# Down biases of a mixture-of-experts layer added as the products leave PSUM, with a new written-out order

## The chip, the cores and the metric

The kernel runs on one core of one Trainium2 chip. A time is the device time of one execution in microseconds (us). The kernel before has three timed executions, with a median of 795.2 us. The engines are TensorE (PE, with its weight loads as PEld), VectorE (DVE), ScalarE (ACT), GpSimd (POOL) and SyncE (SP), which here issues most of the transfers.

## The reference, cut to what matters

A two-layer block on x of 16 sequences, 256 rows each, 128 channels. Layer 0 is attention and a mixture of experts, layer 1 a gated recurrence, a gated feed-forward network and a channel mixer. The change lies in the experts (`I` is 512, `E` is 8, two experts a row):

```python
scores = sigmoid(xf @ gate_w + bias)
top_scores, top_idx = top_k(scores, K)
top_scores = top_scores / (sum(top_scores) + 1e-06)
w = zeros((T, E)).at[arange(T)[:, None], top_idx].add(top_scores)
hact = gelu(einsum('th,ehi->tei', xf, up_w) + up_b)
eo = einsum('tei,eih->teh', hact, down_w) + down_b
combined = einsum('teh,te->th', eo * 0.1, w)
shared = (gelu(xf @ sw_up + sb_up) @ sw_down + sb_down) * 0.1
out = shared + combined
out = out / (max(abs(out)) + 1e-06)
```

## The kernel before, in words

The 4096 rows are 8 chunks of 512. The program has four stages.

1. Attention, chunk by chunk, with the second layer norm, the routing and the scatter of rows to the experts of the chunks that are done. It ends where DVE writes the last residual (`woh`, L1333); SP waits for it before it loads anything late.
2. Expert tiles 0 to 16. A tile is 256 rows of one expert. SP fetches its up and down weights and its rows (`fetch`, L2037 to L2049: buffers WU, WD and XT, six of each); PE transposes the rows (`xt`, L1065) and DVE copies them; four `up` products (L1079), four GELUs (ACT L1784), four `down` steps of two products (L1098); DVE copies the result out of PSUM (`ev`, L1539), and POOL stores it. The shared expert of chunk 0 runs at the start of this stage.
3. Expert tiles 17 to 38. The up weights and rows are split in two (`wsh` and `xs` on DVE, `wsl` on POOL, L1941), and an `up` step is three products (L1085 to L1087).
4. Rest: POOL gathers the expert rows of a chunk back (`gather`, L1963, four steps one after the other), DVE sums and normalizes them (`cmb`, `fin1`), PE transposes (`fin2`, L1113), and layer 1 of that chunk follows. The shared expert of chunks 1 to 7 (`up` L1075, `down` L1098) lies between, as work that waits for no gather.

The shared expert's PSUM bank of a chunk also collects all down biases. `rows` transposes the chunk's routing weights, with a column of ones, to nine rows (L1057: four transposes, copied by ACT at L1772), and after the last `down` step four products over these nine rows (L1105) add the eight expert biases, weighted, and the shared bias. DVE then copies the bank (L1535).

The order is written out. Each program step is a stage of a job; `arrange` reads the strings ORDER1 (stages 1 and 2) and ORDER2 (stage 4), two characters a step, and puts the steps down in that order; each engine runs its own in that order. Stage 3 is written by a loop. While it reads, `arrange` replays the steps with the durations in HELD, the delays in HOPS and BEHIND, and lets `fill` put idle products (L855, no one reads them) where it sees PE too little busy.

Of the kernel before, what the change touches and what calls it, by code (L numbers as in the profile page):

```python
# [7 lines left out]
F = mybir.dt.float32  # L8
R = mybir.dt.float32r
B16 = mybir.dt.bfloat16  # L10
ALU = mybir.AluOpType
# [5 lines left out]
CH = 512  # L17
# [21 lines left out]
def constants():  # L39
# [48 lines left out]
    "up": ("PE", 0.858, None), "rows": ("PE", 0.436, None), "down": ("PE", 0.888, None), "ev": ("DVE", 0.6, None),  # L88
# [18 lines left out]
BEHIND = {"PE": 0.165, "ACT": 0.115, "DVE": 0.08, "POOL": 0.045, "SP": 0.0}  # L107
# [7 lines left out]
def cost(name, key):  # L115
    engine, held, table = HELD["t_" + name if key[:1] == ("t",) else name]
    if name == "mxr" and key[2] == 0:
        held = 0.845
    if name == "causal" and key[1] > 3:
        held = 1.19  # L120
    if name == "pv" and key[2]:
        held = 0.44
    if name == "down" and key[0] == "s" and key[2] == 3:
        held = 1.776
    return engine, held, table
# [29 lines left out]
    "GpG4F2GwGpF3GvGwGpG1GpGvG5GwG5GpGpG6GvG2F3G6GxGqGpG6G7GqG7G9G7G9G6GpGuG3G8G7G+G8G-G+G8G-F3G+G8G-HBG+GzHAG-G8HBHAG8GuGvHC"
    "HAHDHCHAHDF3HCG0HEHDHFHCHEHDHAHEHAHFGuHGHEHHHGG1HIHHGrHGHIHHHJHGHIHHHIHJGvHEG2HKHIHEGvHLHKHIHMHLGrHKHMHLHNHKHNHMHLHOHMHP"
# [153 lines left out]
def schedule():  # L310
# [126 lines left out]
    def plan(n):  # L437
# [3 lines left out]
        if n:  # L441
            yield stage("plan_rows", after=[("woh", NB - 1)])
# [1656 lines left out]
```

## Time and profile before

| what | value |
|---|---|
| three timed executions | 793.75, 795.2, 796.96 us |
| the profiled execution | 796.7 us |
| its span, first to last instruction | 795.0 us |
| mean granted clock of PE | 0.971 |
| busy: PE, DVE, ACT, POOL | 730.2, 502.4, 498.3, 387.8 us |

### The profile page before, as it was taken

The numbers are of one execution on the slowest core, as the hardware profiler recorded it, in microseconds if no ns is written. First come the engines' busy times: TensorE is split into PE (matmuls) and PEld (weight loads), VectorE is DVE, ScalarE is ACT, GpSimd is POOL, SyncE is SP. The second block draws the span as 40 slices with busy tenths as digits, with TensorE's granted clock in tenths as the row PEclk, the third lists the DMA queues.
The fourth block names the chain that finished last, engine by engine and source line by source line (L and its number), as shares of the span: only waits on it lengthen the run. The fifth ranks groups of instructions, "written<-read, shape, count | busy, mean of one in ns | idle before, by whom it ended". The sixth has DMA issues, their size and how long they took to land.

```text
span 795.0 us, 12566 instructions
## 1 busy us (share of the span) xinstructions
PE 730.2 (92%) x3768; PEld 442.7 (56%) x3768; DVE 502.4 (63%) x1906; ACT 498.3 (63%) x749; POOL 387.8 (49%) x563
## 2 busy tenths in 40 slices
PE   4889899899889998988999899998999999999994
PEld 3444445444544544446789899986545644434442
DVE  3387888879984889784912345513346495795652
ACT  1749675775838556655455455552688886688563
POOL 7327444664856277653451355534445465522243
PEclk9999998999999989899999999998999999999998
DMA  9990000000000000005767667711000101000012
GB/s 280 380 369 29 1 1 0 18 12 14 14 24 4 2 28 24 3 15 168 231 214 214 179 204 233 208 40 31 26 25 23 31 22 32 20 1 0 1 40 66
DMA packets 59855, 64.18 MB, mean 81 GB/s; under 512 B 6474, under 2 KB 42668, under 8 KB 59788
## 3 DMA queue, kind: packets, MB, share of 16 engines
q1 hardware_dynamic: 53410, 49.84, 20.3%
q0 software_dynamic: 6320, 13.53, 5.4%
q8 instruction: 30, 0.49, 0.3%
q14 instruction: 37, 0.30, 0.1%
q10 hardware_dynamic: 58, 0.02, 0.0%
HBM read 35.18 MB, written 28.18 MB: 80 GB/s over the span
## 4 chain that ended last, share of the span: by engine, by line
PE 61%; DVE 15%; issue 8%; POOL 6%; ACT 6%; DMA 3%; SPq 0%; DVEq 0%; POOLq 0%; ACTq 0%
PE PS L1098 11%; DVE JK L1290 6%; PE PS L1079 4%; PE PS L952 3%; PE PS L990 3%; PE PS L1161 3%; PE PS L895 3%; PE PS L1154 3%; PE PS L1168 2%; PE PS L901 2%; POOL got L1963 2%; PE PS L907 2%; DMA got<-expert_out,IG 2%; PE PS L975 2%; PE PS L961 2%
## 5 line engine op out<-in xcount | busy, mean ns | idle before, releaser
L1290 DVE CUSTOM_DVE_ANT_0 JK<-PS,CM 128x256 bf16<-128x256 f32 (+1 forms) x512 | 148.9, 352 | 23.3 <-PE PS L952 21.9
L1784 ACT ACTIVATE GF<-PS,XN 128x256 f32<-128x256 f32 x156 | 73.7, 475 | 67.1 <-PE PS L1087 37.4
L1098 PE MATMUL PS<-WD,GF 128*128 128x128 f32 x624 | 94.9, 276 | 0.9 <-ACT GF L1784 0.6
L952 PE MATMUL PS<-KZ,QS 128*128 128x512 f32 x192 | 87.2, 506 | 5.5 <-DVE MX L1290 3.0
L1963 POOL DMA_INDIRECT got<-expert_out,IG x64 | 63.6, 993 | 54.4 <-DMA got<-expert_out,IG 38.2
L1098 PEld LDWEIGHTS PS<-WD,GF 128*128 128x128 f32 x624 | 85.9, 192 | 6.4 <-ACT GF L1784 1.9
L1935 POOL DMA_INDIRECT expert_rows<-five,IU x64 | 63.1, 986 | 50.2 <-DMA expert_rows<-five,IU 20.4
L1738 ACT ACTIVATE PA<-PS 128x1024 f32<-128x1024 f32 x64 | 64.1, 1029 | 21.7 <-PE PS L975 21.4
L1922 POOL TENSOR_SCALAR_AFFINE_SELECT PA<-PA 128x256 f32<-128x256 f32 x128 | 50.0, 420 | 52.1 <-ACT PA L1738 50.7
L1885 POOL TENSOR_SCALAR H<-xc,MOD 128x256 f32<-128x256 f32 x56 | 32.9, 598 | 79.4 <-DVE xc L1259 79.3
L952 PEld LDWEIGHTS PS<-KZ,QS 128*128 128x128 f32 x192 | 35.6, 197 | 43.9 <-DVE MX L1290 20.7
L1946 POOL DMA_DIRECT2D expert_out<-YT x39 | 21.7, 557 | 68.8 <-DVE YT L1539 68.1
L1922 POOL TENSOR_SCALAR_AFFINE_SELECT PB<-PB 128x512 f32<-128x512 f32 x64 | 39.5, 645 | 18.9 <-ACT PB L1740 18.7
L1290 DVE DVE_READ_ACCUMULATOR2_ANT MX<- 128x1 f32 x512 | 42.3, 83 | 0.0
L1079 PE MATMUL PS<-XS,WU 128*128 128x256 f32 x136 | 41.2, 385 | 1.0 <-DVE XN L1535 0.5
L1606 DVE SCALAR_TENSOR_TENSOR hf<-PS,V,GF 128x512 f32<-128x512 f32 x32 | 23.7, 745 | 28.1 <-PE PS L1161 25.4
L1098 PEld LDWEIGHTS PS<-five,GF 128*128 128x128 f32 x256 | 33.8, 196 | 11.8 <-issue 10.8
L1740 ACT ACTIVATE PB<-PS 128x1024 f32<-128x1024 f32 x32 | 32.5, 1027 | 7.2 <-PE PS L977 5.8
L895 PE MATMUL PS<-X,CT 128*128 128x512 f32 x64 | 35.4, 636 | 1.5 <-DVE X L1333 1.4
L901 PE MATMUL PS<-sq,CT 128*128 128x512 f32 x58 | 32.4, 644 | 4.4 <-DVE MX L1290 1.8
L990 PE MATMUL PS<-PA,VA 128*32 128x512 f32 x256 | 34.3, 629 | 2.2 <-DVE MX L1290 0.5
L1539 DVE COPY YT<-PS 128x256 f32<-128x256 f32 x39 | 16.5, 424 | 31.1 <-PE PS L1098 31.1
(295 smaller groups left out, 1741.6 us busy)
## 6 DMA issues: line engine op xcount, KB each, us to landing
expert_rows<-five SPq DMA_DIRECT2D x16, 1024.0 KB, 12.8
WU<-in_L_ffn_up_w SPq DMA_DIRECT2D x39, 256.0 KB, 2.9
WD<-in_L_ffn_down_w SPq DMA_DIRECT2D x39, 256.0 KB, 3.1
XT<-expert_rows SPq DMA_DIRECT2D x39, 128.0 KB, 3.2
expert_out<-YT POOLq DMA_DIRECT2D x39, 128.0 KB
PA<-in_L_attn_x SPq DMA_DIRECT2D x8, 256.0 KB, 5.5
out<-yo SPq DMA_DIRECT2D x8, 256.0 KB, 2.3
expert_rows<-five,IU POOLq DMA_INDIRECT x64
```

What stands on the lines that cost most here:

```text
L895: pe.matmul(bank("lc", c, s), centre, chunk(X, c), start=True, stop=True).then_inc(sems["cen"], 1)
L901: pe.matmul(bank("ln_var", c, s), mean, sq_of("sq", c, s), start=True, stop=True).then_inc(sems["var"], 1)
L952: pe.matmul(bk.rearrange("p (j n) -> p j n", n=wd), q, ks, start=True, stop=True).then_inc(sems["mx_mm"], 1)
L990: m = pe.matmul(o, VA[:, 2 * b % 8, j, :], p0[:, j, 2 * h:2 * h + 2, :], start=True, stop=False)
L1079: pe.matmul(bk[:, 0:TR], WU[u % NF][:, f], XS[slot["xs", u]][:, :], start=True, stop=True).then_inc(sems["up"], 1)
L1098: m = pe.matmul(bk[:, b], g[:, b], wd[:, k, :], start=(k == 0 and t == 0), stop=(k == 3 and t == TB - 1 and kind == "t"))
L1290: m = dve.tensor_tensor_reduce(JK[n % 2][:, s], bk[:, s], CM[:, 256 - wd:256] if wd == 128 else CM[:, 0:256], -1.0, 3.0e38, ALU.add, ALU.m ...
L1738: m = act.activation(PT0[b % 2][:, j:j + 2, g:g + 2, :].rearrange("p j g n -> p j (g n)"), two(both), ACT.Exp, scale=SCALE)
L1784: act.activation(GF[slot["gf", kind, u, k]][:, 0:n], bank("up", kind, u, k)[:, 0:n], ACT.Gelu, bias=bias).then_inc(sems["gelu"], 1)
L1922: m = pool.affine_select(out=a, in_=a, pattern=[[0, 2 if u < 4 else 4], [1, 128]], compare_op=ALU.is_ge, fill=zero, base=0, channel_multip ...
L1935: pool.indirect_dma_start(out=XD[:, :], out_offset=bass.IndirectOffsetOnAxis(ap=IU[:, c, n, k:k + 1], axis=0), in_=HT[c % 2][:, k, :], in_ ...
L1963: pool.indirect_dma_start(out=got[b][n][:, k, :], out_offset=None, in_=YD[:, :], in_offset=bass.IndirectOffsetOnAxis(ap=IG[:, n, 4 * c + k ...
```

## The change

The nine rows go: `rows`, its ACT copy, the four products over them, their buffers WT and DB. Each expert tile gets a buffer BD, six in all: `fetch` loads the expert's down bias, the same 512 bytes to each of 128 partitions, between WD and XT, and the tile's semaphore counts to 64 in place of 48. `ev` adds BD as it leaves PSUM. The shared bias is loaded once in the same way (SD), ahead of the late weights, and the shared `ev` adds it. A fetch waits for the `ev` of the tile six before, which was a wait for its last `down`. Both order strings are new, and BEHIND holds 0.25 for PE, which was 0.165, and 0.12 for ACT, which was 0.115.

```diff
-BEHIND = {"PE": 0.165, "ACT": 0.115, "DVE": 0.08, "POOL": 0.045, "SP": 0.0}
+BEHIND = {"PE": 0.25, "ACT": 0.12, "DVE": 0.08, "POOL": 0.045, "SP": 0.0}
...
-    "H3H5H2H5H4H3H6H4H7H6H4G2H8H7H4H6H8H7H6H8H7H8H8G3H8"
+    "H6H4H6H4H4H4H6H6H7H7H7H7G4H8H8H8H8G2GzG0G1H8H8G3"
...
-            yield stage("plan_rows", after=[("woh", NB - 1)])
+            yield stage("plan_rows", after=[("woh", NB - 1), ("rt_out", NCH - 1)])
...
-                        + ([("down", "t", t - NF, 3)] if t >= NF else []))
+                        + ([("ev", "t", t - NF)] if t >= NF else []))
...
-                if k == 1:
-                    yield stage("rows", c, takes=[(ring, "rows", (c,), ("rw", c)), (WTS, "wts", (c,), ("down", "s", c, 3))])
...
-                            after=[("gelu", "s", c, k)] + [("load_late",)] * (k == 3))
+                            after=[("gelu", "s", c, k)])
...
-        yield stage("ev", "s", c, after=[("down", "s", c, 3)])
+        yield stage("ev", "s", c, after=[("down", "s", c, 3), ("load_late",)])
...
-    WT = [sb(f"WT{k}", [9, CH]) for k in range(2)]
-    DB = sb("DB", [9, 128])
+    SD = sb("SD", [128, 128])
+    BD = [sb(f"BD{k}", [128, 128], where=moe) for k in range(NF)]
...
-            if kind == "s" and k == 3:
-                w.wait_ge(*at("rw", u))
-                w.wait_ge(ld_db, 32)
-                for t in range(4):
-                    b = slice(128 * t, 128 * t + 128)
-                    m = pe.matmul(bk[:, b], WT[slot["wts", u]][:, b], DB[:, :], start=False, stop=(t == 3))
+                              stop=(k == 3 and t == blocks - 1))
...
-                dve.tensor_copy(chunk(XN, u), bank("down", kind, u)).then_inc(sems["ev"], 1)
+                w.wait_ge(ld_sd, 16)
+                dve.tensor_tensor(shared(u), bank("down", kind, u).rearrange("p (k d) -> p k d", d=128),
+                                  SD[:, :].unsqueeze(1).to_broadcast([128, 4, 128]), ALU.add).then_inc(sems["ev"], 1)
...
-            dve.tensor_copy(YT[u % 3][:, :], bank("down", kind, u)[:, 0:TR]).then_inc(sems["ev"], 1)
+            dve.tensor_tensor(YT[u % 3][:, :].rearrange("p (k d) -> p k d", d=128),
+                              bank("down", kind, u)[:, 0:TR].rearrange("p (k d) -> p k d", d=128),
+                              BD[u % NF][:, :].unsqueeze(1).to_broadcast([128, TB, 128]), ALU.add).then_inc(sems["ev"], 1)
...
-            sp.dma_start(DB[0:8, :], i["L0_ffn_down_b"]).then_inc(ld_db, 16)
-            sp.dma_start(DB[8:9, :], i["L0_ffn_sb_down"].rearrange("(a p) -> a p", p=128)).then_inc(ld_db, 16)
+            sp.dma_start(SD[:, :], i["L0_ffn_sb_down"].partition_broadcast(128)).then_inc(ld_sd, 16)
...
-                w.wait_ge(*at("down", "t", t - NF, 3))
+                w.wait_ge(*at("ev", "t", t - NF))
...
+            sp.dma_start(BD[k][:, :], i["L0_ffn_down_b"][bass.ds(ex, 1)].rearrange("o h -> (o h)").partition_broadcast(128)
                         ).then_inc(ld_t[k], 16)
```

The order moves on every engine. Three places follow. A row is a line of the program, the operation, what it writes and reads, and its shape; "x4" stands for four in a row. Line numbers are lower by 4 to 23 in the kernel after.

First, PE from the shared `up` and `down` steps of chunk 3 to the first `fin2` (the one that reads `on`), while the first gather is under way. Before:

```order
L1098 MATMUL PS<-five,GF 128x128 x4
L1075 MATMUL PS<-H,five 128x512
L1057 MATMUL PS<-CT,WS 9x128 x4
L1098 MATMUL PS<-five,GF 128x128 x4
L1075 MATMUL PS<-H,five 128x512
L1098 MATMUL PS<-five,GF 128x128 x4
L1105 MATMUL PS<-DB,WT 128x128 x4
L1075 MATMUL PS<-H,five 128x512
L1113 MATMUL PS<-CT,on 128x128 x4
```

After:

```order
L1085 MATMUL PS<-five,GF 128x128 x4
L1062 MATMUL PS<-H,five 128x512
L1085 MATMUL PS<-five,GF 128x128 x4
L1062 MATMUL PS<-H,five 128x512
L1085 MATMUL PS<-five,GF 128x128 x4
L1062 MATMUL PS<-H,five 128x512
L1094 MATMUL PS<-CT,on 128x128 x4
```

Between the last tile and the first `fin2` PE had 12 `up` and 8 `down` steps, three times the nine-row transposes and two times the nine-row products; it now has 13 `up` and 9 `down` steps.

Second, SP at the change from the second to the third stage, from the fetch of tile 17 (buffer 5) to the next one. Before:

```order
L2044 DMA WU5<-in_L0_ffn_up_w 128x512
L2045 DMA WD5<-in_L0_ffn_down_w 128x4x128
L2049 ISA
L2049 DMA XT5<-expert_rows 128x256
L2042 TENSOR_LOAD XN
L2042 ISA x2
L2043 TENSOR_LOAD XN
L2043 ISA x2
L2044 ISA
L2044 DMA WU0<-in_L0_ffn_up_w 128x512
```

After:

```order
L2021 DMA WU5<-in_L0_ffn_up_w 128x512
L2022 DMA WD5<-in_L0_ffn_down_w 128x4x128
L2024 ISA
L2024 DMA BD5<-in_L0_ffn_down_b 128x128
L2028 ISA
L2028 DMA XT5<-expert_rows 128x256
L2019 TENSOR_LOAD XN
L2019 ISA x2
L2020 TENSOR_LOAD XN
L2020 ISA x2
L2021 ISA
L2021 DMA WU3<-in_L0_ffn_up_w 128x512
```

The fetch that follows that of tile 17 was that of tile 18 (buffer 0); it is now that of tile 21 (buffer 3), and those of tiles 18, 19, 20 and 22 come behind it. The fetch of tile 21 waits for tile 15.

Third, PE where the tiles begin, from the weight transposes (`gates`) to the first expert `up` (the one that reads `WU`). Before:

```order
L1122 MATMUL PS<-CT,gates 128x128 x2
L1098 MATMUL PS<-five,GF 128x128 x4
L1122 MATMUL PS<-CT,gates 128x128 x4
L1065 MATMUL PS<-CT,XT 128x128 x2
L1098 MATMUL PS<-five,GF 128x128 x4
L1105 MATMUL PS<-DB,WT 128x128 x4
L1079 MATMUL PS<-XS,WU 128x256
```

After:

```order
L1103 MATMUL PS<-CT,gates 128x128 x2
L1052 MATMUL PS<-CT,XT 128x128 x2
L1021 MATMUL PS<-gate,H 128x8 x4
L1030 MATMUL PS<-CT,H 128x128 x4
L1103 MATMUL PS<-CT,gates 128x128 x4
L1066 MATMUL PS<-XS,WU 128x256
L1085 MATMUL PS<-five,GF 128x128 x4
L1066 MATMUL PS<-XS,WU 128x256
```

Three of the four shared `down` steps of chunk 0 now lie between the `up` steps of tile 0, and the routing of chunk 7 lies ahead of them. Over the whole program `fill` puts 18 idle products in the place of 50.

## Rows read from the trace of the kernel before

**Rows 1.** Windows: span, busy time (instructions) per engine, PE clock, DMA share, GB/s

```profile
0.00:361.50 361.50, 320.81 (x1728) 167.46 (x1728) 279.73 (x1422) 229.14 (x331) 203.47 (x355) 0.96 0.20 67
480.00:500.00 20.00, 20.00 (x178) 20.00 (x177) 10.20 (x24) 10.92 (x23) 10.58 (x12) 1.00 0.79 235
528.00:552.00 24.00, 21.50 (x118) 14.44 (x116) 5.02 (x15) 9.30 (x15) 10.24 (x11) 0.97 0.13 37
552.00:586.00 34.00, 31.53 (x135) 19.63 (x135) 12.63 (x28) 22.30 (x27) 12.96 (x15) 0.87 0.09 24
586.00:795.00 209.00, 196.93 (x586) 94.12 (x584) 131.92 (x239) 150.11 (x200) 93.19 (x104) 0.99 0.08 24
```

**Rows 2.** The page: the chain that ended last, by engine

```profile
PE 61%; DVE 15%; issue 8%; POOL 6%; ACT 6%; DMA 3%; SPq 0%; DVEq 0%; POOLq 0%; ACTq 0%
```

**Rows 3.** Timeline of PE in stage 4: start, duration, line, tiles, records

```profile
605.98 1.05 PE L1098 MATMUL PS<-five,GF 128*128 128x128 f32 x8
606.97 1.15 PE L1105 MATMUL PS<-DB,WT 9*128 9x128 f32 x8
...
609.01 1.02 PE L1075 MATMUL PS<-H,five 128*128 128x512 f32 x2
609.87 1.02 PE L1147 MATMUL PS<-bz,WL 128*128 128x512 f32 x2
610.73 1.05 PE L1098 MATMUL PS<-five,GF 128*128 128x128 f32 x8
611.62 1.02 PE L1168 MATMUL PS<-hf,WL 128*128 128x512 f32 x2
...
618.10 0.60 PE L1057 MATMUL PS<-CT,WS 128*9 128x128 f32 x4
618.54 1.02 PE L1154 MATMUL PS<-XN,WL 128*128 128x512 f32 x2
```

**Rows 4.** Timeline of PE as the first gather ends

```profile
548.37 1.13 PE L1075 MATMUL PS<-H,five 128*128 128x512 f32 x2
552.34 1.12 PE L1113 MATMUL PS<-CT,on 128*128 128x128 f32 x4 [2.84 <-DVE on L1570]
```

**Rows 5.** Timeline of SP: fetch issues in stage 2, and of tile 21

```profile
371.93 0.34 SPq L2044 DMA_DIRECT2D WU<-in_L_ffn_up_w  x1
372.39 0.38 SPq L2045 DMA_DIRECT2D WD<-in_L_ffn_down_w  x1
...
374.65 0.33 SPq L2044 DMA_DIRECT2D WU<-in_L_ffn_up_w  x1
...
447.33 0.36 SPq L2049 DMA_DIRECT2D XT<-expert_rows  x1
```

**Rows 6.** Issue to landing of the row fetches XT

```profile
DMA to landing us min/median/max: 2.9/3.2/4.1
```

**Rows 7.** Timeline of PE: the rows of tile 18

```profile
452.23 0.63 PE L1065 MATMUL PS<-CT,XT 128*128 128x128 f32 x2
```

**Rows 8.** Groups of instructions: the idle products

```profile
L855 PE MATMUL PS<-CT 128*128 128x128 f32 x100 | 18.9, 299 | 0.0
```

**Rows 9.** Windows: a stretch of attention at the lower clock

```profile
130.00:135.00 5.00, 3.94 (x8) 2.23 (x9) 4.03 (x20) 2.62 (x5) 2.76 (x7) 0.58 0.00 0
```

**Rows 10.** Groups of instructions on DVE by form

```profile
L1539 DVE COPY YT<-PS 128x256 f32<-128x256 f32 x39 | 16.5, 424 | 31.1 <-PE PS L1098 31.1
L1521 DVE TENSOR_TENSOR XL<-PS,XH 128x256 fp32r<-128x256 f32 x22 | 9.3, 424 | 0.8
L1276 DVE TENSOR_TENSOR qt<-PS,CT 128x512 f32<-128x512 f32 x8 | 5.5, 686 | 5.7 <-PE PS L915 5.7
L1535 DVE COPY XN<-PS 128x512 f32<-128x512 f32 x8 | 5.5, 684 | 17.4 <-PE PS L1105 17.4
```

**Rows 11.** SP's waits for PE: total, times, longest

```profile
SPq L2042 <- PE PS L1098: 30.1, 27, 6.3
```

**Rows 12.** The page: the software queue's packets, MB, share of 16 engines

```profile
q0 software_dynamic: 6320, 13.53, 5.4%
```

More of the change, by code:

```diff
@@ L87 @@
     "plan_rows": ("DVE", 4.9, None), "fetch": ("SP", 2.9, None), "load_late": ("SP", 3.0, None), "tw": ("PE", 0.4, None),
-    "up": ("PE", 0.858, None), "rows": ("PE", 0.436, None), "down": ("PE", 0.888, None), "ev": ("DVE", 0.6, None),
+    "up": ("PE", 0.858, None), "down": ("PE", 0.888, None), "ev": ("DVE", 0.6, None),
     "gelu": ("ACT", 0.57, "gelu"), "t_up": ("PE", 0.434, None), "t_gelu": ("ACT", 0.36, "gelu"), "t_down": ("PE", 0.444, None),
@@ L298 @@
     "pl_ei": "plan_tiles", "pl_ub": "plan_bias", "pl_ix": "plan_rows", "pl_w": "plan_rows",
-    "rw_tp": "rows", "rw": "rows", "xt_tp": "xt", "xs": "xs", "w_hi": "wsh", "w_lo": "wsl", "up": "up", "gelu": "gelu", "down": "down", "ev": "ev",
+    "xt_tp": "xt", "xs": "xs", "w_hi": "wsh", "w_lo": "wsl", "up": "up", "gelu": "gelu", "down": "down", "ev": "ev",
     "cmb": "cmb", "fin": "fin1", "fin_bk": "fin2", "moe_x": "fin3", "cen": "lc",
@@ L316, in schedule @@
     LT, LH, LL, LN = (Ring(range(2)) for _ in range(4))
-    GF, WTS, XS, WS2 = Ring(range(6)), Ring(range(2)), Ring(range(2)), Ring(range(2))
+    GF, XS, WS2 = Ring(range(6)), Ring(range(2)), Ring(range(2))
     def stage(name, *key, takes=(), after=()):
@@ L1049, in dpm @@
             m.then_inc(sems["dp_mm"], 1)
-        def rows(c):
-            w.wait_ge(*at("wst", c))
-            w.wait_ge(zeroed, 4)
-            for e in prior["rows", c]:
-                w.wait_ge(*at(*e))
-            for k in range(4):
-                m = pe.transpose(bank("rows", c)[0:9, 128 * k:128 * k + 128], WS[:, c, k, :], ident)
-            m.then_inc(sems["rw_tp"], 1)
         def xt(t):
-            w.wait_ge(ld_t[t % NF], 48 * (t // NF + 1))
+            w.wait_ge(ld_t[t % NF], 64 * (t // NF + 1))
             for e in prior["xt", t]:
@@ L1765, in hta @@
             act.activation(HT[c % 2].rearrange("p k d -> p (k d)"), bank("ht", c), ACT.Copy).then_inc(sems["ht"], 1)
-        def rows(c):
-            w.wait_ge(*at("rw_tp", c))
-            w.wait_ge(*at(*att_done))
-            for e in prior["wts", c]:
-                w.wait_ge(*at(*e))
-            act.activation(WT[slot["wts", c]][:, :], bank("rows", c)[0:9, :], ACT.Copy).then_inc(sems["rw"], 1)
         def gelu(kind, u, k):
```

106 lines of the change are left out of this document (52 added, 54 removed).

## The prediction

> **What bounds the kernel now.** I read the windows by stage first. In stage 4, from 586 us, PE is busy for 196.93 of 209 us, DVE for 131.92 and ACT for 150.11 [rows 1]; stage 3 is full too, 20.00 of 20. The reader is to see that these stretches are paid for in PE time: what PE has less to do there comes off the end, unless something else comes late. Attention is looser: PE 320.81 of 361.5 us, and DVE 279.73 [rows 1]. The chain that ended last says the same, 61% over PE [rows 2]. Between 528 and 552 us PE has shared work only while the first gather runs, and then stands 2.84 us for the normalized rows of chunk 0 [rows 4]. The clock goes with such stands: 0.58 of full speed in 130 to 135 us [rows 9], a mean of 0.87 over the 34 us behind the first gather [rows 1].
>
> **What a chunk's nine rows cost PE.** A shared `down` step followed by another kind of product takes 0.89 us from start to start (610.73 to 611.62), a 512-column product 0.86 (609.87 to 610.73) [rows 3]. With the nine-row products between, `down`, nine rows and the next product take 609.01 - 605.98 = 3.03 us; without them it would be 0.89 + 0.86 = 1.75. So the four products cost 1.28 us, not just their own 1.15, since the neighbours on both sides are drawn out. The four transposes cost 618.54 - 618.10 = 0.44 [rows 3]. One chunk is 1.72 us, eight are 13.8.
>
> **Stage 4.** Seven chunks lie here, 12.0 us. Two products and three sets of transposes stood ahead of the first `fin2`, 3.9 us of cover for the gather. The new order puts one more `up` (0.86) and one more `down` (0.89) in, so cover falls by 2.1 us and the stand grows from 2.84 [rows 4] to about 5: no gain and no loss, the gather sets that time. Behind it five products and four sets of transposes go, 5 x 1.28 + 4 x 0.44 = 8.2, and the two steps moved ahead, 1.75. That is -9.9 us. What hid nothing there hides nothing now: after the work of PE the next in line is ACT, at 150.11 of 209 [rows 1]. The ends: -12.0 if every part counts; -4 if PE starves behind the first gather, where it already had 2.5 us idle of 34 [rows 1] and now has some 6 us less shared work to fill in.
>
> **Start of stage 2.** One set of nine rows, 1.72 us, goes from between the end of attention and the tiles. Tile 0's fetch is now the first of its kind rather than the second, but the new transfer stands ahead of its rows, and the second layer norm and routing of chunk 7 stand ahead of its first `up` on PE. I take -1.7, between -4 (a whole fetch of 2.72 us, 371.93 to 374.65 [rows 5], gained as well) and +2 (that much lost to chunk 7, less the nine rows).
>
> **Change to stage 3: a wait is added.** SP now fetches tile 21 ahead of tile 18. In the trace the rows of tile 21 are issued at 447.33, behind tile 15 [rows 5]. The new fetch starts some 0.5 later (it waits for `ev`, a copy of 0.42 [rows 10] with its signal, and not for the last `down`), has one more issue of 0.46 (371.93 to 372.39), and only then comes tile 18's, 2.72 + 0.46 = 3.18 [rows 5]: rows issued at 451.5, landed 3.2 later [rows 6], 454.7. PE transposed them at 452.23 [rows 7]. Behind that transpose stand the last two `up` steps and all `down` steps of tile 17, and `wsh` on DVE and `wsl` on POOL wait for the same load. So PE stands 2.5 us: +2.5. It is 0 if the gap that is already there before tile 17 reaches over it, 3.5 if the split of the weights comes late too. The fetches of tiles 19 and 20 follow at 3.2 us, and PE takes a tile per 3.4 us (12 `up`, 16 `down` and 2 transpose records make 30; 178 records in 20 us [rows 1]), so they only just arrive.
>
> **The two additions that I cost at nothing.** DVE: the copy out of PSUM takes 424 ns for 256 columns and 684 for 512; an addition of a PSUM and an SBUF operand 424, and with a broadcast middle dimension 686 [rows 10]. SP and the transfers: SP waited 27 times for PE ahead of a fetch, 30.1 us, 1.1 a time [rows 11]; the new issue and the later signal take about 1.0 of it, and a fetch is six tiles ahead. The DMA engines are busy 0.79 of 3.37 us a tile [rows 1], 2.66 us. A tile moves 768 KB in 896 pieces (WU 128, WD 512, XT 128, YT 128); 64 KB in 128 pieces more is 0.22 by bytes, 0.38 by pieces, so at most 3.04 of 3.37. What hides it is gone if a piece costs as one of the software queue, 5.4% of 16 x 795 us over 6320 [rows 12], 109 ns: 0.87 a tile, 3.53 in all, 0.16 over, times 22 tiles +3.5 us. I take 0.
> The Trainium skill ("DMA: Bandwidth & Descriptors", section "Bandwidth") speaks against the transfer: in its words, "Transfers under 64 KB are descriptor-dominated", and this one is just at that size, in rows of 512 bytes. Its rule would put the sum nearer the end of +3.5 us, the row of bytes nearer 0; it is the third rival.
>
> **Attention.** No part of the nine rows is here; only the order and the idle products change. In the trace the 50 idle products make 100 records [rows 8]; two records are a quarter of the 0.89 us of a `down` step, 0.22 us. 32 fewer are 7.0 us of PE if none stood in a gap, and 0 if all did. PE has 40.7 us without work in attention [rows 1], so a better order has room, and the order says nothing of what it does on the chip. I take -3, with -12 (a third of that gap) and +12 (below) as ends.
>
> **The sum.** -9.9 - 1.7 + 2.5 - 3 + 0 = -12.1. Against the profiled execution, 796.7 us: 784.6. That execution is 1.5 above the median of 795.2, so for the median 783.1; I say 783.5. The likeliest case alone runs from 776 to 789.
>
> **Rivals.**
> First, the one on the other side: the clock. The idle products go from 50 to 18, and each longer stand in attention is followed by a stretch at 1.2 GHz. 130 to 135 us lost 0.42 x 5 = 2.1 us [rows 9], and such a stretch has its ends in the neighbouring windows, so up to 3.4. If six more such stretches come, that is up to +20: 803.5. It decides from about four more (13.6 us eat up the -12.1). For it: the mean clock is already 0.96 there with the idle products. Against: most of them stand in small gaps, and they go where the planner sees none.
> The Trainium skill ("TensorE: Matmul & The Clock Gate", section "HAM oscillation — how this bites in real kernels") has it that an array which idles between bursts of work is throttled anew and pays at the half clock; by that this rival has the mechanism, and the stretch at 0.58 agrees.
> Second, stage 4 is bound by the gathers and by the chain of a chunk for longer, so that the shared work is missed: the -9.9 shrinks to -4 and the sum to -6, 789. For: PE waits for the first gather now. Against: from 586 us on it waits for nothing.
> Third, the biases' transfers fill the DMA engines, or the new fetch order costs again at each tile 18 to 20: +3.5, 787. For: 0.79 busy. Against: six buffers.
> Fourth, the new order is worth in attention and behind the first gather what its room allows: -12 there, and 2 more: 772.
>
> **Chances.** Forecast 0.57, clock 0.13, gathers 0.13, transfers 0.04, better order 0.13. A measurement of this kernel tells 0.5%, 4 us, from no change. Faster than 791.2: nearly all of the forecast, three in four of the second and third rival, all of the fourth, 0.78; I lower it to 0.75, as an order is hard to judge from its rows. Within 0.5%: 0.12. Slower than 799.2: 0.13. The range runs from 773 to 798: it leaves out half of the fourth rival and most of the first.
>
> **What would show it.** Right: no records of nine-row products or transposes; stage 4 from the last tile to the end shorter by about 10 us, with PE still full behind some 590 us; the stand before the first `fin2` near 5 us; DVE additions at 424 and 686 ns; a stand of 2 to 3 us at the transpose of tile 18; tiles of stage 3 still at 3.4 us. Wrong: attention longer by more than 4 us with more windows below a clock of 1; idle PE between 560 and 620 us; SP without waits and the DMA share near 1 in stage 3; or the stages each as said but attention by 10 us shorter.

## The result, and the profile after

The changed kernel takes 772.1 us (median; single executions 762.7 to 774.0) against 796.0 us (the profiled execution of 796.7 us counted in), a ratio of 0.968 (95% interval 0.961 to 0.975). Executions over 1.5% above the shortest of their kernel are left out of every ratio below, among them one of the changed kernel in r4 that took 1139.3 us at a mean granted clock of 0.557, for which nothing here gives a cause. The forecast was 783.5 with a range of 773 to 798: the direction was right, the gain of 24 us is twice the 12.1 forecast, and the median lies just below the range. The profiled execution is the shortest one, 762.7 us with a span of 760.9, so its stages are set below beside those of other executions.

The windows of the changed kernel: attention; tiles 17 to 38; shared work until the first `fin2`; the 34 us behind it; the rest; and 20 us of stage 3. Columns as in [rows 1].

```profile
0.00:334.20 334.20, 302.43 (x1671) 155.98 (x1671) 284.38 (x1424) 226.84 (x331) 204.27 (x355) 0.99 0.22 73
426.30:506.90 80.60, 77.37 (x659) 77.17 (x660) 35.67 (x84) 41.69 (x88) 38.87 (x42) 0.96 0.73 216
506.90:532.40 25.50, 19.21 (x99) 12.62 (x98) 4.70 (x15) 8.24 (x12) 10.24 (x11) 0.95 0.12 32
532.40:566.00 33.60, 31.55 (x131) 19.63 (x132) 13.17 (x28) 24.17 (x31) 16.65 (x19) 0.94 0.10 28
566.00:760.90 194.90, 183.70 (x522) 86.94 (x520) 131.65 (x238) 135.25 (x186) 91.00 (x99) 0.99 0.09 25
480.00:500.00 20.00, 20.00 (x177) 20.00 (x176) 9.95 (x24) 10.94 (x24) 10.54 (x13) 1.00 0.67 199
```

Attention ends at 334.2 instead of 361.5 us [rows 1], with VectorE busy for 284 us (280 before). PE is busy there for 18.4 us less and idle for 31.8 us instead of 40.7. The chain of the page (before: [rows 2]) has moved towards VectorE, which answers for 22% in place of 15%:

```profile
PE 56%; DVE 22%; issue 7%; ACT 5%; DMA 4%; SPq 2%; POOL 2%; DVEq 0%; ACTq 0%; POOLq 0%
```

The stages of both profiled executions, in us. Attention ends with VectorE's last residual; stage 3 runs from the second product of tile 17 (0.2 us behind the first, where the window above begins) to the last `down` of tile 38.

| | attention | stage 2 | stage 3 | shared work to first `fin2` | rest | span |
|---|---|---|---|---|---|---|
| before | 361.5 | 89.9 | 76.8 | 24.2 | 242.6 | 795.0 |
| after | 334.2 | 92.3 | 80.4 | 25.5 | 228.5 | 760.9 |
| forecast of the difference | -3 | -1.7 | +2.5 | -9.9 for the last two together | | -12.1 |
| measured | -27.3 | +2.4 | +3.6 | +1.3 | -14.1 | -34.1 |

Three single rows of the forecast can be read directly. The first two are on PE (timeline, columns as in [rows 4, 7]): the rows of tile 18, then the first `fin2`.

```profile
430.48 0.69 PE L1052 MATMUL PS<-CT,XT 128*128 128x128 f32 x2 [3.23 <-DMA XT<-expert_rows]
...
532.37 1.11 PE L1094 MATMUL PS<-CT,on 128*128 128x128 f32 x4 [6.29 <-DVE on L1556]
```

PE stands 3.23 us for tile 18 (2.5 forecast) and 6.29 us ahead of the first `fin2` (5 forecast). The SP timeline gives the reason for the first as it was forecast: the fetch of tile 21 is issued first, that of tile 18 behind it, and its rows land after 430 us.

```profile
423.87 0.33 SPq L2028 DMA_DIRECT2D XT<-expert_rows  x1
...
427.06 0.33 SPq L2028 DMA_DIRECT2D XT<-expert_rows  x1
```

The groups of instructions answer to [rows 8] and [rows 10]: the idle products have 36 records, not 100; the two additions take 424 and 683 ns, as the copies did.

```profile
L851 PE MATMUL PS<-CT 128*128 128x128 f32 x36 | 6.9, 338 | 0.0
...
L1523 DVE TENSOR_TENSOR YT<-PS,BD 128x256 f32<-128x256 f32 x39 | 16.5, 424 | 46.5 <-PE PS L1085 46.5
...
L1518 DVE TENSOR_TENSOR XN<-PS,SD 128x512 f32<-128x512 f32 x8 | 5.5, 683 | 3.9 <-PE PS L1085 3.8
```

The hardware queue of the page carries 59152 packets, where it had 53410; 39 x 128 = 4992 of the 5742 more are the tiles' biases:

```profile
q1 hardware_dynamic: 59152, 52.46, 22.8%
```

### The profile page after: what moved, and what is told of

It reads as the page before. It is cut to its first block, busy times and chain, and to the rows that moved or that the text cites. A ratio compares the mean times of both kernels' runs of the same rounds, so it can differ in the third digit from the quotient of the medians.

```text
span 760.9 us, 12350 instructions
## 1 busy us (share of the span) xinstructions
PE 696.3 (92%) x3608; PEld 424.0 (56%) x3608; DVE 505.9 (66%) x1906; ACT 481.8 (63%) x734; POOL 388.6 (51%) x562
## 3 DMA queue, kind: packets, MB, share of 16 engines
q1 hardware_dynamic: 59152, 52.46, 22.8%
## 4 chain that ended last, share of the span: by engine, by line
PE 56%; DVE 22%; issue 7%; ACT 5%; DMA 4%; SPq 2%; POOL 2%; DVEq 0%; ACTq 0%; POOLq 0%
PE PS L1085 9%; DVE JK L1271 8%; PE PS L948 4%; PE PS L1135 3%; PE PS L891 3%; PE PS L986 3%; PE PS L1066 3%; PE PS L1149 3%; PE PS L1142 3%; PE PS L897 2%; PE PS L903 2%; PE PS L988 2%; PE PS L911 1%; DMA got<-expert_out,IG 1%; PE PS L1072 1%
## 5 line engine op out<-in xcount | busy, mean ns | idle before, releaser
L1724 ACT ACTIVATE PA<-PS 128x1024 f32<-128x1024 f32 x64 | 64.7, 1026 | 15.2 <-PE PS L971 14.1
L1900 POOL TENSOR_SCALAR_AFFINE_SELECT PA<-PA 128x256 f32<-128x256 f32 x128 | 49.8, 419 | 27.9 <-ACT PA L1724 27.3
L1924 POOL DMA_DIRECT2D expert_out<-YT x39 | 21.7, 558 | 80.3 <-DVE YT L1523 80.3
L1523 DVE TENSOR_TENSOR YT<-PS,BD 128x256 f32<-128x256 f32 x39 | 16.5, 424 | 46.5 <-PE PS L1085 46.5
L1900 POOL TENSOR_SCALAR_AFFINE_SELECT PB<-PB 128x512 f32<-128x512 f32 x64 | 38.9, 635 | 16.4 <-ACT PB L1726 16.2
L1085 PEld LDWEIGHTS PS<-five,GF 128*128 128x128 f32 x256 | 34.7, 198 | 14.1 <-issue 12.7
L1653 ACT ACTIVATE sq<-PS 128x512 f32<-128x512 f32 x28 | 16.7, 599 | 31.4 <-PE PS L891 31.2
L1534 DVE SCALAR_TENSOR_TENSOR XN<-got,W,XN 128x128 f32<-128x128 f32 x64 | 20.8, 386 | 21.8 <-DMA got<-expert_out,IG 21.5
L1085 PE MATMUL PS<-five,GF 128*128 128x128 f32 x256 | 35.0, 281 | 0.0
```

What stands on the lines that cost most here:

```text
L1085: m = pe.matmul(bk[:, b], g[:, b], wd[:, k, :], start=(k == 0 and t == 0), stop=(k == 3 and t == blocks - 1))
L1724: m = act.activation(PT0[b % 2][:, j:j + 2, g:g + 2, :].rearrange("p j g n -> p j (g n)"), two(both), ACT.Exp, scale=SCALE)
L1900: m = pool.affine_select(out=a, in_=a, pattern=[[0, 2 if u < 4 else 4], [1, 128]], compare_op=ALU.is_ge, fill=zero, base=0, channel_multip ...
```

## The experiments

Theory A: most of the gain is the new order of attention; the biases and the other orders nearly cancel. Theory B: the nine rows are what was gained. Each table of orders is changed as a whole; of such a diff the first line pair stands here, and the words say what it does. The kernel before was timed with each group of runs (797.0, 797.3, 799.9, 798.9 and 797.3 us), and ratios are to it.

**r1, the changed biases with the old order.**

```diff
-BEHIND = {"PE": 0.25, "ACT": 0.12, "DVE": 0.08, "POOL": 0.045, "SP": 0.0}
+BEHIND = {"PE": 0.165, "ACT": 0.115, "DVE": 0.08, "POOL": 0.045, "SP": 0.0}
...
-    "AFAAAAAAAAABAGAGABACAAAAAAABADABAEABABABAAAAAGAGAHAHAAAAAAAKAKAGAGAGABABALALANANAGANANAMAMAMAMAJABABAJABAHAHAPAPAQAQAOAO"
+    "AAAAACABAFAAABADAAAAABAEABAGAGABAAAAAKABALABAAAKAGALABAIAAAJAGAAAIAJAGAAABAHAAAIAGAHAGANAIAGAMANANABAMANAMAHABATAHAMABAP"
```

> The changed biases, with the order of the kernel before (its steps of the nine rows taken out, its planner numbers kept, so 36 fill steps with 60 idle products where the kernel before has 50 with 100). Theory A (most of the gain is the new order in attention, some 27 us of the two profiled executions): attention ends within 5 us of the 361.5 us of before, stage 4 is shorter by about 10 us, and the time is about 785 us. Theory B (the removal of the nine rows is worth most, the order little): about 775 us. If idle products cost PE time (rival C), attention is shorter by up to 9 us too (40 fewer products of 0.22 us).

(The counts of idle products there are wrong: the kernel before has 35 steps with 50 products, recorded as 100, and this one 36 steps with 60.) Measured: 787.8 us, ratio 0.990 (0.982 to 0.998), some 8 us. The profiled execution took 800.9 us, 13 more than the median, and attention ends at 372.9 us in it, not within 5 us of 361.5 as expected; most of that is a slow start and the clock (below). Stage 3 takes 76.8 us as before, though every tile fetches its bias, so the transfer costs nothing. Behind the first `fin2` it takes 236.0 us instead of 242.6: the five chunks of nine rows there are worth 6.6 us, not the 8.2 forecast, and 1.7 of the 6.6 are the clock (a stretch of 3.4 us at 1.2 GHz that the kernel before has at 581 us does not come).

**r2, the old attention in the changed kernel; r3, the new attention in the kernel before.** r2 exchanges the table up to the residual of block 15 and the planner numbers, r3 the same the other way round (the diff of r1 in reverse, on the kernel before).

> The changed kernel with the old order up to the end of attention, the new order behind it. Theory A: attention ends near 361 us again, the time is 772 + 20 to 27 = 792 to 799 us. Theory B: within 5 us of the changed kernel, 767 to 777 us. The stage behind the last tile keeps the 254 us of the changed kernel by both.

> The kernel before (biases as products over nine rows) with the new order up to the end of attention, the old order behind it; 9 fill steps in place of 50. Theory A: attention ends at 334 to 340 us, the time is 796 - 20 to 27 = 769 to 776 us. Theory B: 790 us or more. What lies behind attention keeps its 433.5 us (361.5 to 795.0) by both.

Measured: r2 792.1 us, ratio 0.989 (0.978 to 1.000), attention 367.6 us in the profiled execution; r3 773.5 us, ratio 0.969 (0.960 to 0.978), attention 334.9. Both times lie where theory A puts them. (The 50 steps in r3's expectation are 35.) r3 has none of the change of the biases and has its whole gain. Its windows, attention and all from the last tile's last `down` on:

```profile
0.00:334.90 334.90, 301.60 (x1671) 155.58 (x1671) 283.30 (x1423) 226.77 (x331) 204.44 (x356) 0.99 0.22 73
...
505.30:771.90 266.60, 249.70 (x835) 128.00 (x833) 149.63 (x280) 181.69 (x242) 116.19 (x129) 0.97 0.09 25
```

The last part is the 266.8 us of before. (Of the expectation's 433.5 us behind attention it takes 437.0; the 3.5 more lie in stage 2.) Theory A holds, B falls.

**r4, the changed kernel again.** No edit.

> The changed kernel once more, word for word, since its executions lie up to 11 us apart (762.7 to 774.0). If one stage is what varies, the profile shows it: a time near 772 us with attention ending some 9 us later than 334 us means that it is attention and its clock; a later stage longer by 9 us means that it is that one.

Measured: 768.9 us. The profiled execution is 8.0 us longer than the first one, and attention is 7.4 us longer (341.6), with stretches at the lower clock of 27.3 us in all where the first had 6.8. What differs between these two executions lies in attention.

**r11, all new orders, with the nine rows.**

```diff
-BEHIND = {"PE": 0.165, "ACT": 0.115, "DVE": 0.08, "POOL": 0.045, "SP": 0.0}
+BEHIND = {"PE": 0.25, "ACT": 0.12, "DVE": 0.08, "POOL": 0.045, "SP": 0.0}
...
-    "AAAAACABAFAAABADAAAAABAEABAGAGABAAAAAKABALABAAAKAGALABAIAAAJAGAAAIAJAGAAABAHAAAIAGAHAGANAIAGAMANANABAMANAMAHABATAHAMABAP"
+    "AFAAAAAAAAABAGAGABACAAAAAAABADABAEABABABAAAAAGAGAHAHAAAAAAAKAKAGAGAGABABALALANANAGANANAMAMAMAMAJABABAJABAHAHAPAPAQAQAOAO"
```

> All new orders (attention, tiles, fetches, the second layer), with the biases of the shared expert as products over nine rows as before. If the parts add up (measured so far, in profiled executions: attention -17 to -27, stage 2 +2.4, stage 3 +4, the last part -8 of its -14), the time is 770 + 6 to 9 = 776 to 779 us, and the bias change by itself is worth 6 to 9 us. Rival: the nine rows fill gaps before the first gather and chunk 0 and are worth 3 us at most, 770 to 773.

Measured: 770.0 us, ratio 0.961 (0.954 to 0.969), against 0.968 and 0.961 of the changed kernel. In the new order the change of the biases can't be told from nothing: the rival is right. Its windows from the last tile on, until the first `fin2` and behind it:

```profile
512.80:536.80 24.00, 23.11 (x127) 15.57 (x125) 4.63 (x15) 8.37 (x14) 10.24 (x11) 1.00 0.12 35
536.80:768.70 231.90, 220.72 (x708) 111.41 (x708) 144.20 (x266) 161.85 (x221) 107.21 (x118) 0.99 0.09 25
```

Ahead of the first `fin2` PE is idle for 0.9 us of 24.0, at the full clock, where the changed kernel is idle for 6.3 of 25.5. No stretch at the lower clock follows, where the changed kernel has one of 6.8 us (0.95 ahead of the first `fin2`, 0.94 over the 34 us behind it). In this order the nine rows filled that gap. The whole part is 255.8 us with them and 254.0 without: without them PE is busy for 9.3 us less there, but idle for 7.5 us more (19.5 against 12.0).

**Where attention gains: r9, the new order up to block 4; r10, the new order from there on.** Both are the kernel before with the old order behind attention. r9 has the first lines of r11's diff, the new planner numbers with them; r10 keeps the old numbers:

```diff
-    "CMCzCyCcCzCNCbCNCaCZCyCODFDEC1COCyCZCyCPCcC0C1CPA-CPC0CgCPAIC0C1AIDJCgCZC1CgCaC0DdC2CfDJA-DdC4C3C4DdDGC3CfC+DdDGCfC6DIDH"
+    "CMCzCyCcCzCNCbCNCaCZCyCODFDEC1COCyCZCyCPCcC0C1CPA-CPC0CgCPAIAIDcDcDdDdDdDcDcBxBxC1C1C0C0CZC2BxBxDdCaCvCvC3C3DJDJDeDeC4C4"
```

> The kernel before with the new order up to the residual of attention block 4 (about 160 us), and the old order of all that is left behind it. By then the new order has started 646 instructions on VectorE where the old one has 582. Theory of the head start (what is brought forward on VectorE early is harvested at the end of attention): 797 - 8 to 15 = 782 to 789 us. Rival (the gain accrues where the order is denser, and the first 160 us are the part without a gain): within 4 us of the kernel before, 793 to 801 us.

> The counterpart: the kernel before with the old order up to the residual of block 4, the new order from there to the end of attention, the old one behind it. Head start: 797 - 8 to 15. Rival: nearly all of it, 797 - 18 to 23 = 774 to 779 us.

Measured: r9 789.7 us, ratio 0.987 (0.979 to 0.996); r10 792.3, ratio 0.988 (0.979 to 0.996). Each half is worth 8 to 10 us, the whole 23. r9's gain of 10 us is the size that the theory of the head start gave, and the rival (the first 160 us bring nothing, the rest nearly all) falls in both runs. In the profiled executions attention ends at 351.6 us in r9, 9.9 sooner than in the kernel before; 6.8 of these are the clock (13.7 us at 1.2 GHz instead of 27.3) and 3.6 idle time of PE. In r10 it ends at 361.5, as before, but with 41.0 us at the lower clock; that execution (796.4 us) is also 4 us above r10's median.

**r14, the changed kernel with the old planner numbers**, which choose banks and idle products.

```diff
-BEHIND = {"PE": 0.25, "ACT": 0.12, "DVE": 0.08, "POOL": 0.045, "SP": 0.0}
+BEHIND = {"PE": 0.165, "ACT": 0.115, "DVE": 0.08, "POOL": 0.045, "SP": 0.0}
```

> The changed kernel with its orders and the old planner numbers (0.165/0.115), which give 426 of its 1685 buffers another place and 8 idle-product steps instead of 7. If the order is the cause: 768 to 774 us, attention within 5 us of 334 to 341. If the choice of banks is: towards 790.

Measured: 765.3 us, ratio 0.956 (0.949 to 0.963), attention 338.8. It is the order, not the banks: the time is not above the changed kernel's.

**The idle products: r5, none in the changed kernel; r6, 48 instead of 18; r13, none in the kernel before.** r5 and r13 share the first edit.

```diff
 def fill(P, banks, done, busy, since, until, own):
+    return until
```

```diff
-WINDOW, LEAST, WORST, MOST, ONE, SPARE = 3.4, 0.6, 0.5, 2, 0.215, 0.1
+WINDOW, LEAST, WORST, MOST, ONE, SPARE = 3.4, 0.7, 0.65, 3, 0.215, 0.1
```

> The changed kernel without any idle products (7 steps with 18 products go). If an idle product only costs its time (0.22 us each), attention ends up to 4 us sooner and the time is 766 to 770 us. If the idle products hold the clock (the rival of the prediction), attention shows two or more further stretches of 7 us at half the clock and the time is 775 us or more.

> The changed kernel with the planner's thresholds for idle products raised (0.6/0.5/2 to 0.7/0.65/3), the order of all other work kept: 36 steps with 48 products, about as many as the kernel before has (35 with 50). If part of what attention gained is that 32 idle products went, it is longer by up to 7 us (775 to 779); if they stand in gaps and hold the clock, it is 765 to 771.

> The kernel before without its 50 idle products. If they cost their time (0.22 us each, with the neighbours), it is faster by up to 11 us, 786 to 792; if they fill gaps and hold the clock, slower by 4 us or more, 801 to 810, with more than 27 us at half the clock in attention. From the changed kernel (18 products taken out moved nothing) I expect within 4 us of 797.

Measured: r5 772.9 us, ratio 0.967 (0.962 to 0.973); r6 767.1, ratio 0.961 (0.956 to 0.966); r13 807.3, ratio 1.007 (1.002 to 1.011). In the profiled executions r5 has 41.0 us at the lower clock in attention, r6 6.8. Taking all 50 out of the kernel before costs 5 us by the ratio and 8 by the medians: the second case of the expectation, and my "within 4 us" falls. Its 34.1 us at the lower clock alone would not show why, since r10 has 41.0 with 36 idle products, but the mean granted clock of all executions does: 0.948 to 0.961 without them, 0.963 to 0.980 for the kernel before timed beside it. In the changed kernel neither direction leaves the spread of its own executions, but r5 and r6, timed together, do not overlap: four executions of 770.3 to 775.1 us at clocks of 0.957 to 0.969 without idle products, four of 765.7 to 768.0 at 0.979 to 0.981 with 48. That is r6's second case, while r5 falls between its two, and it is about 6 us for 48 idle products here too. So 32 fewer idle products are not what gained 23 us, and the premise of the clock rival, that they hold the clock, is right in both kernels.

**r7 and r16, the fetch of tile 21 behind those of 18 to 20.** One table line; the letter pairs `Gz` and `G0` to `G3` are the fetch jobs.

```diff
-    "H6H4H6H4H4H4H6H6H7H7H7H7G4H8H8H8H8G2GzG0G1H8H8G3"
+    "H6H4H6H4H4H4H6H6H7H7H7H7G4H8H8H8H8GzG0G1G2H8H8G3"
```

> The changed kernel with the fetch of tile 21 behind those of tiles 18 to 20 again. By the step of the prediction the stand of 3.2 us at the transpose of tile 18 goes, and with it perhaps the low-clock stretch behind it: the stretch of tiles 17 to 38 falls from 80.4 to 81.1 us to about 77, the time by 3 to 4 us, to about 768. Rival: the stand comes back at tile 21, and nothing is gained.

> The fetch order's repair alone once more, on the chip of r15: 760 to 764 us. If r15 is within 2 us of it, the repair of the late weights is worth nothing in the whole, though its stage got 4 to 5 us shorter.

Measured: r7 761.6 us, ratio 0.953 (0.947 to 0.958); r16 764.3, ratio 0.956 (0.949 to 0.962). Stage 3 in r7 and the transpose of tile 18, which now waits for nothing:

```profile
433.60:508.90 75.30, 75.30 (x659) 75.29 (x659) 35.20 (x83) 41.61 (x88) 39.07 (x42) 1.00 0.72 209
```

```profile
434.16 0.38 PE L1052 MATMUL PS<-CT,XT 128*128 128x128 f32 x2
```

75.3 us (76.5 in r16) against 80.4 and 81.1 in the changed kernel, whose order costs 4 to 5 us here: the stand and a stretch at the lower clock behind it. Of the two, r16 (expected 760 to 764) is the second timing of the same kernel, so the repaired kernel is at 762 to 764 us, where 768 was expected.

**r8, the first fetch ahead of the late weights, and the transposes of those weights behind tile 1; r12, this and the fetch order; r15, r12 with the idle products of r6; r17, all fetches in the order of the tiles, the late weights behind the fetch of tile 1.** The jobs moved are `Gs` (late weights) and `Gv` (their transposes). r8:

```diff
-    "GSGSGRGRGtF0F0F0F0GjGkGjGjGkGkGTGTGmGmGlGlGTGTFDGnGnF1F1F1GnGnF1F1F1F1F1F3F3GoGwGwGoGoGyGyGsGzG0G3G1G2F2F2GoGoGoGwGwGwGv"
+    "GSGSGRGRGtF0F0F0F0GjGkGjGjGkGkGTGTGmGmGlGlGTGTFDGnGnF1F1F1GnGnF1F1F1F1F1F3F3GoGwGwGoGoGyGyGzGsG0G3G1G2F2F2GoGoGoGwGwGwGy"
```

> The changed kernel with the first tile's fetch ahead of the late weights on SP, and the transposes of those weights on PE behind tile 1. The fetch of tile 0 is then issued at about 334 rather than 341 us, and the stands of 2.3 and 2.6 us on PE at 344 and 347 us go: 4 to 5 us less, up to 8 if the low-clock stretch at 345 to 352 goes too; 765 to 768 us. Rival: the same products wait for chunk 7's routing instead, and under 2 us are gained.

> The changed kernel with both repairs: fetches in order for tiles 18 to 21, and the first tile's fetch ahead of the late weights. If they add (about -8 and -5), 757 to 760 us, with tiles 0 to 16 at 87 us and tiles 17 to 38 at 75 to 77. Rival: they free the same wait, 762.

> Both repairs, and 48 idle products rather than 18. If the idle products only steady the clock, 758 to 763 us and a narrower spread than the 8.7 us of r12; if they cost, 765 or more.

> The changed kernel with all fetches in the order of their tiles and the late weights behind the fetch of tile 1 (the transposes of those weights behind tile 1 on PE, as in r8). If the stand at tile 1 was what the repair still cost, tiles 0 to 16 take 84 to 85 us (87.1 in r8, 92.0 in the changed kernel), tiles 17 to 38 75 to 77, and the time is 756 to 760 us. Rival: PE waits for tile 2 or for the shared bias instead, and the stage stays at 87 to 89 us: 761 to 764.

Measured: r8 765.8 us, ratio 0.962 (0.955 to 0.968); r12 762.9, 0.953 (0.944 to 0.962); r15 764.0, 0.954 (0.947 to 0.961); r17 762.0, 0.954 (0.947 to 0.962). r8 is as expected (765 to 768); r12 and r17 came out where their rivals put them, at 762 to 763, and not at the 757 to 760 and 756 to 760 of the repairs added up. In r8 two stands of the changed kernel went, 2.3 and 2.6 us,

```profile
344.13 0.41 PE L1103 MATMUL PS<-CT,gates 128*128 128x128 f32 x2 [2.29 <-DMA gates<-in_L_attn_w_out]
347.11 0.66 PE L1052 MATMUL PS<-CT,XT 128*128 128x128 f32 x2 [2.56 <-ACT GF L1763]
```

and PE stood at tile 1 instead:

```profile
352.86 0.44 PE L1052 MATMUL PS<-CT,XT 128*128 128x128 f32 x2 [2.92 <-DMA XT<-expert_rows]
```

The 87.1 us that r17's expectation gives for r8 was misread: it ran from SP's late issue, which this edit moves. From the last residual, stage 2 takes 90.7 us in r8, 91.5 in r12, 89.4 in r17 and 92.1 in r4. This repair is worth 1 to 3 us of its stage and cannot be seen in the whole. The versions with the fetch order put right (r7, r12, r15, r16, r17) lie at 762 to 764 us, between 4 and 5% faster than the kernel before and about 1% faster than the changed one.

## Why the prediction was right and wrong

**Attention, -3 forecast (ends -12 and +12), 20 to 27 measured in the profiled pairs (r4, after): the step that failed.** "-12 (a third of that gap)" took the room from PE's idle time alone, 40.7 us (a third would be 13.6). But the 320.8 us of busy PE held room as well. The table puts two profiled executions in the old order (before and r2; r1's is far above its median and left out) beside the twelve in the new order with idle products (after, r3, r4, r6 to r8, r11, r12, r14 to r17):

| means, us | old | new |
|---|---|---|
| attention | 364.5 | 338.6 |
| PE idle | 42.0 | 33.8 |
| time at 1.2 GHz, and half of it as the loss | 22.2, 11.1 | 10.0, 5.0 |

So some 26 us of attention (23.5 in whole times for r3). Of the 26, 8.2 are idle time, about 6 the clock, and up to 7 the 32 idle products at the 0.22 us of the forecast (attention of r6 and r15, which have them again, is 3 to 5 us longer than the mean of the others, 337.9, but their whole times are not). Some 3 more come from the start of the program: its first 12 products for the modulation take 1.41 us in the kernel before as profiled, but 2.58 in r1, r2, r10 and r13, which begin with the old order too. The two timelines, of before and of r1:

```profile
14.82 1.41 PE L870 MATMUL PS<-scT,PA 128*128 128x16 f32 x12
...
20.57 0.27 PE L879 MATMUL PS<-CT,vin 64*128 64x64 f32 x1
```

```profile
14.80 2.58 PE L866 MATMUL PS<-scT,PA 128*128 128x16 f32 x12
...
25.92 0.37 PE L875 MATMUL PS<-CT,vin 64*128 64x64 f32 x1
```

Only profiled executions show it, so how much of the 23.5 us of whole time is this start stays open, and r9's 10 us, which begins with the new order, may hold some of it.

Where the idle time came from shows in VectorE's waits. First before, then after: the waits of VectorE for the attention's products, us in total, times, longest.

```profile
DVE JK L1290 <- PE PS L952: 21.9, 27, 2.8
DVE RC L1319 <- PE PS L1001: 7.2, 8, 2.0
DVE QM L1311 <- PE PS L961: 7.0, 6, 4.5
```

```profile
DVE RC L1300 <- PE PS L997: 5.7, 5, 3.1
DVE JK L1271 <- PE PS L948: 5.7, 14, 0.9
...
DVE QM L1292 <- PE PS L957: 3.1, 5, 1.1
```

The maxima (`JK`) wait 16.2 us less for their products. VectorE's work, 280 to 284 us, is the second floor of this stage (the least time that it can take), and it is fed earlier. First before, then after, 0 to 80 and 80 to 160 us, columns as in [rows 1]:

```profile
0.00:80.00 80.00, 63.50 (x292) 35.05 (x293) 47.56 (x236) 47.32 (x73) 41.39 (x84) 1.00 0.77 263
80.00:160.00 80.00, 72.71 (x394) 35.97 (x393) 66.39 (x346) 53.88 (x77) 39.93 (x72) 0.96 0.02 6
```

```profile
0.00:80.00 80.00, 66.97 (x302) 35.75 (x306) 53.26 (x281) 46.92 (x73) 41.63 (x83) 0.98 0.77 263
80.00:160.00 80.00, 75.83 (x436) 38.64 (x436) 70.75 (x367) 58.51 (x85) 40.82 (x74) 1.00 0.02 5
```

By 160 us VectorE has begun 645 instructions instead of 581 (an instruction that crosses 80 us is counted in both windows), 114 us of work before and 124 after. r9 has this head start (638) and gains 10 us; r10 has none (554) and gains about as much. So the head start can be part of the cause and is not the whole, and that it is what r9 gained by is argued, not shown. Shown is that the order of attention gains the 23 us (r2, r3), in both of its halves. Which single moves matter was not separated.

The fourth rival had this mechanism (the new order is worth in attention "what its room allows") but put it at 12 us with a chance of 0.13. So the term that was mis-sized is the -3 for attention, with its end of -12: r3 measures it alone at -23.5 us.

**The nine rows and stage 4, -9.9 forecast, -12.8 in the profiled pair.** The number is near, its parts are not. The nine rows give 6.7 us in the old order (r1: 260.0 for 266.8) and 1.8 in the new one (255.8 to 254.0); the rest, up to 11 us, is the new order (r11: 255.8 with all nine rows). Of these 11, 5.0 are idle time of PE (12.0 us instead of 17.0) and 5.1 the clock (10.2 us of stretches at 1.2 GHz around and behind the first `fin2` in the kernel before, none in r11). The forecast counted the moved steps alone, 1.75, and for the nine rows all of PE's time for them; that a gap would open where they stood was the second rival's case. Its stand of 5 us came as 6.3: "no gain and no loss" ahead of the gather was wrong by 1.3 us. The clock over the 34 us behind it is 0.94, better than the 0.87 of before [rows 1], but not the 1.00 of r11. That the sum of this stage is near is luck.

**Stage 2, -1.7 forecast, +2.4 measured.** In the old order the nine rows gave 0.4 us (r1: 89.5). The new attention costs the stage behind it: r3, without any change there, takes 93.6 us. Its fetches start 1.4 us later, as SP's issue of `attn_w_out` among the late weights takes 2.13 us instead of 0.50; PE stands 3.7 us for the rows of the first tiles (none before), and a stretch of 10.2 us at the lower clock begins in that stand. The changed kernel stands twice, 2.3 and 2.6 us, and has 6.8 us at the lower clock. Why it comes with the new attention was not separated.

**Stage 3, +2.5 forecast, +3.6 measured.** Right in place and cause; the stand is 3.2 us instead of 2.5. The clock adds little to the difference: the changed kernel has 6.8 us at 1.2 GHz here, 3.0 of them within the stand, and the kernel before has 3.4 too, behind its stand of 2.5 us ahead of tile 17. r7 and r16 take the stand away, and r7 has no stretch at the lower clock here at all, hence its 75.3 us against the 76.8 of before. In r7 no later transpose of rows waits 0.2 us or more: tiles 19 to 21 arrive in time, as said.

**Costs at nothing: right.** VectorE's additions cost no more than copies. The transfers are hidden: r1 has them with stage 3 at 76.8 us. Per tile they take 0.3 us of the DMA engines (the hardware queue's share goes from 20.3% of 795.0 us to 21.7% of 799.2 in r1, 12 us over 39 tiles), between the bounds of 0.22 and 0.38. The forecast took the share of 0.79 from 20 us; over all of stage 3 it is 0.60 before and 0.66 in r1, so there was more room than it counted. What they do cost is time to landing: a tile's rows land 3.7 us after their issue in r1 and in the changed kernel, 3.2 before, and six buffers hide that. The Trainium skill ("DMA: Bandwidth & Descriptors", section "Bandwidth") says of transfers under 64 KB that they are dominated by their descriptors, and these are just at that size; whether they are, no run here shows, but in this trace the engines have room for them.

**The clock rival, wrong in its outcome, right in its premise.** It expected more stretches at 1.2 GHz with fewer idle products. Idle products do hold the clock (r13; r5 against r6), but the new order had 10.0 us at 1.2 GHz in attention on average where the old had 22.2. Nor does each longer stand bring such a stretch: those of 1.4 us at 129.7 and 216.9 us in the kernel before are followed by one, that of 1.6 us at 112.7 us in the changed kernel is not.

**The sum.** All stages behind attention together gave 6.8 us (6.2 in r4) for the 9.1 forecast. What the forecast lacks is attention alone.

## What to carry to other kernels

An order of work is a change by itself, and may be the greatest part: time it alone and the named change alone, since the named change (8 us in one order, nothing measurable in the other) did not keep its worth. Room in a stage is not only the idle time of its busiest engine: busy time that holds stretches at the lower clock and idle products is room too, and the second engine's waits say whether an order can use it. Work taken from ahead of a wait that nothing else fills is not gained; behind the stand of 6.3 us that opened here the clock went as well. Idle products are worth trying again after a change of order: 48 instead of none were 6 us in the changed kernel. After an order search, look through the few issues that it left out of sequence: one fetch put back was worth 4 to 5 us of its stage.

## What the hardware did that I had not expected

The clock falls with PE full as well. In the changed kernel again (r4) PE is busy for 15.90 of 16 us, and the next 10 us are at the lower clock, half of full speed.

```profile
178.00:194.00 16.00, 15.90 (x76) 9.08 (x76) 15.75 (x97) 13.65 (x20) 13.71 (x22) 0.99 0.06 17
194.00:204.00 10.00, 10.00 (x38) 3.27 (x41) 7.10 (x34) 5.62 (x8) 3.35 (x7) 0.50 0.00 1
```

The first execution of the same kernel is 2 us ahead at this place. It does the same work (97 instructions on VectorE in both), is as full, and stays at the full clock:

```profile
176.00:192.00 16.00, 15.90 (x78) 8.99 (x76) 15.75 (x97) 13.64 (x21) 13.72 (x23) 1.00 0.06 17
192.00:202.00 10.00, 9.56 (x68) 4.36 (x66) 9.76 (x51) 7.97 (x12) 6.03 (x10) 1.00 0.05 16
```

Such stretches go with the 11 us by which the changed kernel's executions differ: the mean granted clock is 0.978 in the shortest (762.7 us) and 0.959 in the longest (774.0). They are also why the first profiled execution is 8 us shorter than the one of r4. A single profiled execution of this kernel is therefore good for a stage's stands and durations, which repeat (stage 3 is 76.8 us in eight of the kernels), and not for the time of attention to better than some 7 us. What decides whether the clock falls there stays open. Nor does a full PE always bring the full clock at once: in r1 PE has no stand from 12.7 to 26.2 us (10.00 busy of the 10 us from 15 to 25), and its products take their long durations until 26.3 us, while in the kernel before, after the same work, they take the short ones from 14.8 us on.
